# Local transformer: a new order of projections, scores, mixtures and gelus on the engines of one core

## The chip, the cores and the metric

The kernel runs on one core of a Trainium2 chip. The metric is the device time of one execution in microseconds (us), the median of several runs.

## The reference

Four layers, each x = x + s(LN(x)) * silu(g(LN(x))), with s an attention and g a feed-forward branch of many kinds. The change lies in the branch g of the first layer alone. That branch is itself a small transformer of 6 layers on 16 sequences of 256 tokens of 128 channels, with local attention:

```python
def attn_layer(x, Wqkv, qs, ksc, Wo):
    q, k, v = heads(x @ Wqkv)                 # 16 heads of 64
    q = l2norm(q) * qs; k = l2norm(k) * ksc
    q, k = rotary(q, scale), rotary(k, 1 / scale)
    out = local_attention(q, k, v)            # windows of 32 queries, 64 keys, softmax
    return out @ Wo

def ffn_layer(x, g, bln, W1, b1, W2, b2):
    hg = (layer_norm(x) * g + bln) @ W1 + b1
    a, gate = split(hg)                       # 341 + 341
    return a * gelu(gate) @ W2 + b2

for i in range(6):
    x = attn_layer(shift_tokens(x), ...) + x
    x = ffn_layer(shift_tokens(x), ...) + x
```

## The kernel before

The function local_transformer_stage works on tiles of 128 tokens: 32 tiles a layer, 192 in all, with all data in float32. It is one software pipeline. Each engine has its own instruction queue, written out as a loop over steps n; in step n, TensorE projects tile n, turns and scores tile n - 2, turns the probabilities of tile n - 3 and mixes it, and sends tile n - 4 through the output projection. Every fourth step carries a part of the feed-forward block for a group of 4 tiles: n mod 4 = 3 turn_rows and copy_rows, 0 the matmuls of gate and value with gelu (hidden, gelu, gate_hidden), 1 measure_rows, project_hidden and store_group. In odd steps turn_x and copy_x bring the input of the next two tiles.

The queues run in order and are joined by semaphores. What ties them around the change:

- A projection (project, L1127) goes in four units Q0, Q1, K0, K1 into a ring of two PSUM banks. ScalarE squares it (L1319), VectorE rotates it (L1522, L1526) and sums the squares (L1530); the bank is free when it is rotated. Gate and value matmuls (L1233) use the same ring.
- There is one PSUM bank for transposes (turn_bank). Each group of four transposes (L1135 for q and k, L1168 for probabilities, L1224 rows, L1117 x) waits until ScalarE has copied the group before it out (L1337, L1377, L1311).
- The scores (L1145 mask, L1158) of a tile fill two banks; VectorE takes the maxima (L1537) and subtracts them (L1542, shift_scores), ScalarE takes exp (L1348), VectorE sums (L1549), GpSimd multiplies by the reciprocals (L1482).
- The mixture (mix, L1183) is done in two pieces into the same two banks; ScalarE copies each piece to u (L1356), and project_out (L1195) multiplies u by the merged weights m, 16 heads of two passes each, into a bank of its own. A float32 matmul shows as two passes, each with a weight load.
- The norms' roots are taken by ScalarE (take_root: log L1342 and exp L1344) and refined by GpSimd (refine_root, L1464 to L1467); GpSimd also adds (L1450) and normalises (L1475).
- ScalarE changes its function table before the gelus (L1383) and back after them (L1390).

The projections and transposes use all 128 rows of TensorE's array; mask, scores and mixture work on halves of 64 rows.

## Time and profile before

| | us |
|---|---|
| median of 3 runs (lowest, highest) | 5391.65 (5387.35, 5395.55) |
| the profiled execution | 5392.81 |
| its span, first to last instruction | 5391.0 |
| TensorE matmuls busy, weight loads busy | 4720.6, 3338.6 |
| VectorE, ScalarE, GpSimd busy | 3708.4, 2807.9, 2810.1 |

Times of instructions are counted from the span's start. The mean clock that TensorE was granted over the span is 0.934 of full speed; in the stretch shown below it is 1.00. Matmuls are pipelined, so that the busy time of one instruction reaches into the next one; distances from start to start tell what a block costs.

### The profile page before, as it was taken

The page shows a single profiled execution, that of the slowest core. Times are in us where ns is not written, and L with a number is a line of the kernel's source. Part 1 is how long each engine was busy: PE and PEld are TensorE (multiplying, and loading weights), DVE is VectorE, ACT ScalarE, POOL GpSimd, SP SyncE. Part 2 cuts the span into 40 slices and gives each one's busy share as a digit, 9 for nine tenths or more (in the row PEclk, how much of TensorE's full clock was granted, in tenths as well). Part 3 has the DMA queues.
Part 4 walks back from the last instruction along what each step waited for, and adds up shares of the span by engine and source line. Part 5 has one row for each costly group of instructions (what it writes and reads, how often), then busy time and mean ns, then how long its engine had stood idle before and what let it go on. Part 6 is the DMA issues. An engine that isn't in the chain of part 4 may idle for free. (4 is left out here: it accounts for less than half of the span.)

```text
span 5391.0 us, 143191 instructions
## 1 busy us (share of the span) xinstructions
PE 4720.6 (88%) x57069; PEld 3338.6 (62%) x57103; DVE 3708.4 (69%) x8589; ACT 2807.9 (52%) x6208; POOL 2810.1 (52%) x3349
## 2 busy tenths in 40 slices
PE   7699999999999999999999999955375999845886
PEld 3367676666667767666676667744363667623665
DVE  7677777777777777777777777746725656577443
ACT  2266666666666666666666666621023666641342
POOL 4477776777677767776777777701122333311000
PEclk9799999999999999999999999977587999967898
DMA  0211111111111111111111110000211000010012
GB/s 21 66 35 25 25 35 37 25 25 33 32 29 25 35 31 29 25 35 33 29 25 34 22 28 21 18 24 2 77 52 24 2 2 2 1 25 13 26 29 58
DMA packets 312165, 150.62 MB, mean 28 GB/s; under 512 B 146143, under 2 KB 301004, under 8 KB 311244
## 3 DMA queue, kind: packets, MB, share of 16 engines
q1 hardware_dynamic: 309451, 137.20, 10.5%
q8 instruction: 461, 7.55, 0.6%
q0 software_dynamic: 2048, 4.20, 0.3%
q14 instruction: 205, 1.67, 0.1%
HBM read 101.10 MB, written 27.41 MB: 24 GB/s over the span
## 5 line engine op out<-in xcount | busy, mean ns | idle before, releaser
L1450 POOL TENSOR_TENSOR loc_a<-loc_a,loc_b 128x512 f32<-128x512 f32 x768 | 977.2, 1272 | 598.3 <-DVE loc_b L1526 598.3
L1127 PE MATMUL psum<-loc_wqk,loc_xt 128*128 128x512 f32 x1536 | 837.6, 628 | 12.3 <-DVE loc_b L1526 5.9
L1195 PE MATMUL psum<-loc_m,xn_rows 128*128 128x128 f32 x6144 | 843.7, 280 | 3.8 <-DVE y_rows L1558 2.6
L1475 POOL TENSOR_TENSOR loc_a<-loc_a,loc_rn 128x512 f32<-128x512 f32 x768 | 784.9, 1043 | 0.1
L1195 PEld LDWEIGHTS psum<-loc_m,xn_rows 128*128 128x128 f32 x6144 | 745.6, 192 | 55.9 <-issue 36.0
L1319 ACT ACTIVATE loc_sq<-psum 128x512 f32<-128x512 f32 x768 | 456.1, 594 | 449.6 <-PE psum L1127 443.2
L1522 DVE TENSOR_TENSOR loc_a<-psum,loc_rope 128x512 f32<-128x512 f32 x768 | 523.9, 682 | 174.9 <-ACT loc_sq L1319 161.7
L1356 ACT COPY xn_rows<-psum 128x512 f32<-128x512 f32 x768 | 412.3, 589 | 326.6 <-PE psum L1183 324.3
L1482 POOL TENSOR_TENSOR xn_cols<-xn_cols,loc_rec 128x512 f32<-128x512 f32 x384 | 392.3, 1042 | 307.5 <-DVE loc_rec L1553 307.5
L1135 PEld LDWEIGHTS psum<-ident,loc_a 128*128 128x128 f32 x3072 | 347.7, 142 | 317.9 <-issue 307.1
L1526 DVE TENSOR_TENSOR loc_b<-psum,loc_rope 128x512 f32<-128x512 f32 x768 | 520.8, 678 | 0.0
L1530 DVE TENSOR_REDUCE loc_n<-loc_sq 128x8 f32<-128x512 f32 x768 | 517.1, 673 | 0.0
L1135 PE MATMUL psum<-ident,loc_a 128*128 128x128 f32 x3072 | 477.0, 278 | 10.4 <-ACT loc_qt L1337 7.2
L769 POOL TENSOR_TENSOR l2a_p<-l2a_p,l2a_rec 128x256 f32<-128x256 f32 (+1 forms) x256 | 211.5, 826 | 441.5 <-DVE l2a_rec L756 441.5
L1183 PE MATMUL psum<-xn_cols,loc_x 64*128 64x256 f32 x3072 | 435.6, 402 | 1.1 <-ACT xn_rows L1356 0.9
L1537 DVE TENSOR_REDUCE loc_top<-psum 128x8 f32<-128x512 f32 x384 | 247.3, 686 | 236.7 <-PE psum L1158 236.7
L1337 ACT COPY loc_kt<-psum 128x512 f32<-128x512 f32 x384 | 224.7, 585 | 306.2 <-PE psum L1135 306.2
L1158 PE MATMUL psum<-loc_kt,loc_qt 64*32 64x64 f32 x24576 | 333.8, 223 | 3.2 <-issue 2.5
L1158 PEld LDWEIGHTS psum<-loc_kt,loc_qt 64*32 64x32 f32 x24576 | 295.0, 105 | 50.8 <-issue 39.6
L1168 PEld LDWEIGHTS psum<-ident,xn_cols 128*128 128x128 f32 x1536 | 181.2, 141 | 225.1 <-issue 225.1
L1127 PEld LDWEIGHTS psum<-loc_wqk,loc_xt 128*128 128x128 f32 x1536 | 232.7, 191 | 122.2 <-issue 59.7
L1183 PEld LDWEIGHTS psum<-xn_cols,loc_x 64*128 64x128 f32 x3072 | 264.4, 186 | 67.2 <-issue 10.4
(370 smaller groups left out, 8532.2 us busy)
## 6 DMA issues: line engine op xcount, KB each, us to landing
loc_x<-loc_shifted SPq DMA_DIRECT2D x192, 256.0 KB, 4.0
loc_shifted<-y_rows SPq DMA_DIRECT2D x144, 64.0 KB
loc_wqk<-in_L_ffn_Wqkv SPq DMA_DIRECT2D x24, 256.0 KB, 3.8
x_rows<-y_rows SPq DMA_DIRECT2D x96, 64.0 KB
x_rows<-y_rows SPq DMA_DIRECT2D x96, 63.5 KB
moe_w<-in_L_ffn_W SPq DMA_DIRECT2D x16, 256.0 KB, 5.0
l3a_qk<-l3a_rot SPq DMA_DIRECT2D x16, 256.0 KB, 2.1
grp_w<-in_L_ffn_W SPq DMA_DIRECT2D x16, 256.0 KB, 4.2
```

Source lines behind the costliest of these rows:

```text
L1127: nc.tensor.matmul(ring("p", i, unit), xt[:, b % 2, t * P:(t + 1) * P], wqk[:, unit * 512:(unit + 1) * 512], start=True, stop=True).then_i ...
L1135: last = nc.tensor.transpose(turn_bank[:, j * P:(j + 1) * P], a[:, (UNITS * i + unit) % (3 * UNITS), j * P:(j + 1) * P], core.ident[:, :])
L1158: last = nc.tensor.matmul(score_bank[h][32 * w:32 * w + 32, 64 * j:64 * j + 64], qt[rows_h, i % 2, j, 32 * w:32 * w + 32], kt[rows_h, b % ...
L1183: last = nc.tensor.matmul(u_bank[h][:, 256 * v:256 * v + 256], x2[rows_h, b % 3, WPT * t + w, :], pt[rows_h, i % 2, :, 32 * w:32 * w + 32] ...
L1195: last = nc.tensor.matmul(y_bank[:, 0:P], u[:, i % 2, h // 2, h % 2, :], m[:, h, :], start=(h == 0), stop=(h == HEADS - 1))
L1319: nc.scalar.activation(sq[:, g % 2, :], ring("p", i, unit), ACT.Square).then_inc(sem["squared"], 1)
L1356: nc.scalar.copy(to, u_bank[h].rearrange("p (w j q) -> p w j q", w=2, j=PAIRS)).then_inc(sem["u_copied"], 1)
L1450: nc.gpsimd.tensor_tensor(part, part, b_[:, g % 2, :], ALU.add).then_inc(sem["added"], 1)
L1475: nc.gpsimd.tensor_tensor(part, part, rn[:, i % 2, 8 * unit:8 * unit + 8].rearrange("p (h e) -> p h e", e=1).to_broadcast([P, 8, DH]), ALU ...
L1522: nc.vector.tensor_tensor(a[:, g % (3 * UNITS), :].rearrange("p (h d) -> p h d", d=DH), src.rearrange("p (h d) -> p h d", d=DH), cos, ALU. ...
L1526: nc.vector.tensor_tensor(b_[:, g % 2, :].rearrange("p (h s d) -> p h s d", s=2, d=32), halves, sin, ALU.mult).then_inc(sem["rotated"], 1)
L1530: nc.vector.tensor_reduce(n2[:, i % 2, 8 * unit:8 * unit + 8], sq[:, g % 2, :].rearrange("p (h d) -> p h d", d=DH), AX.X, ALU.add).then_in ...
```

## The change

The work is the same; its order on four queues changes, and one semaphore is split in two.

- TensorE: both projections of q stand first in a step. The output projection goes in four equal parts of 4 heads, three of them between the transposes of q and k, the last before the second mixture (before: 4, 4, 2 and 6 heads). The three gate and value pairs follow all transposes of q and k in one block. The second projection of k and the second transposes of the probabilities come ahead of the mask; the first mixture comes between the two halves of the scores. turn_rows, turn_values and turn_x now follow the scores.
- ScalarE: take_root comes ahead of the first copy of q, the gelu table is loaded ahead of the second copy of q, the three gelus follow all copies of q and k, and the first mixture is copied right after the second copy of the probabilities. The second mixture's copies are keep_mixed, with the semaphore u_kept.
- GpSimd: refine_root comes ahead of the probabilities' multiplies.
- VectorE: normalise_rows_of comes after the rotations of Q0 and Q1, shift_scores after that of K1.

```diff
+                    if piece == 1:
+                        pe.wait_ge(sem["u_copied"], 2 * (i + 1))
+                    elif i >= 1:
+                        pe.wait_ge(sem["u_kept"], 2 * i)
...
+                def project_out(i, part):
+                    if part == 0:
+                        pe.wait_ge(sem["u_copied"], 2 * (i + 1))
+                        pe.wait_ge(sem["u_kept"], 2 * (i + 1))
...
# TensorE, step n
                     if now(0):
                         project(n, Q0)
+                        project(n, Q1)
                     if now(2):
                         turn_qk(n - 2, "q", 0)
-                    if now(0):
-                        project(n, Q1)
+                    if now(4):
+                        project_out(n - 4, 0)
                     if now(2):
                         turn_qk(n - 2, "q", 1)
                     if now(4):
-                        project_out(n - 4, range(0, 4))
-                    if group_at(n, 12) is not None:
-                        hidden(group_at(n, 12), 0)
+                        project_out(n - 4, 1)
                     if now(2):
                         turn_qk(n - 2, "k", 0)
                     if now(4):
-                        project_out(n - 4, range(4, 8))
-                    if group_at(n, 12) is not None:
-                        hidden(group_at(n, 12), 1)
+                        project_out(n - 4, 2)
                     if now(2):
                         turn_qk(n - 2, "k", 1)
                     if group_at(n, 12) is not None:
-                        hidden(group_at(n, 12), 2)
+                        for c in range(CH):
+                            hidden(group_at(n, 12), c)
                     if now(0):
                         project(n, K0)
                     if now(3):
                         turn_probs(n - 3, 0)
-                    if now(2):
-                        mask_scores(n - 2)
-                        scores(n - 2, range(0, 4))
                     if now(0):
                         project(n, K1)
                     if now(3):
                         turn_probs(n - 3, 1)
                     if now(2):
+                        mask_scores(n - 2)
+                        scores(n - 2, range(0, 4))
+                    if now(3):
+                        mix(n - 3, 0)
+                    if now(2):
                         scores(n - 2, range(4, 8))
-                    if now(4):
-                        project_out(n - 4, range(8, 10))
                     if group_at(n, 11) is not None:
                         turn_rows(group_at(n, 11))
                     for half in range(2):
                         if starts(n, 1 + half) is not None:
                             turn_values(n // NT, half)
-                    if now(3):
-                        mix(n - 3, 0)
                     if n % 2 == 1 and n + 1 < TILES:
                         turn_x((n + 1) // 2)
                     if now(4):
-                        project_out(n - 4, range(10, 16))
+                        project_out(n - 4, 3)
                     if now(3):
                         mix(n - 3, 1)
...
# ScalarE, step n
                         square(n, Q0)
+                    if n - 1 in root_number:
+                        take_root(n - 1)
                     if now(2):
                         copy_turned("q", n - 2, 0)
-                    if n - 1 in root_number:
-                        take_root(n - 1)
                     if now(0):
                         square(n, Q1)
+                    if group_at(n, 12) is not None:
+                        nc.scalar.preload_act_table_set("gelu_and_others")
                     if now(2):
                         copy_turned("q", n - 2, 1)
...
                         copy_turned("p", n - 3, 1)
+                        copy_mixed(n - 3)
...
                         exps(n - 2, 0)
                         exps(n - 2, 1)
                     if now(3):
-                        copy_mixed(n - 3, 1)
+                        keep_mixed(n - 3)
...
# GpSimd, step n
                         clamp(n - 1)
+                        refine_root(n - 1)
                     if now(3):
                         normalise_probs(n - 3, 0)
                         normalise_probs(n - 3, 1)
-                    if n - 1 in root_number:
-                        refine_root(n - 1)
...
# VectorE, step n
-                    if group_at(n, 11) is not None:
-                        normalise_rows_of(group_at(n, 11))
                     if now(0):
                         rotate(n, Q0)
                         rotate(n, Q1)
+                    if group_at(n, 11) is not None:
+                        normalise_rows_of(group_at(n, 11))
...
                         rotate(n, K0)
+                        rotate(n, K1)
                     if now(2):
                         shift_scores(n - 2)
-                    if now(0):
-                        rotate(n, K1)
```

## Rows read from the trace of the kernel before

**Rows 1.** Stretches of four steps, their sum: busy us of each engine

```profile
sum 67.91, PE 67.72 PEld 47.61 DVE 52.66 ACT 42.59 POOL 49.07; mean PE 16.93 PEld 11.90 DVE 13.17 ACT 10.65 POOL 12.27
```

**Rows 2.** Timeline of TensorE's matmuls, end of step 1 and step 2: start, us, engine, line

```profile
2017.85 2.94 PE L1242 MATMUL psum<-loc_w,x_rows 128*128 128x128 f32 x24
2020.63 1.02 PE L1127 MATMUL psum<-loc_wqk,loc_xt 128*128 128x512 f32 x2
...
2024.32 0.61 PE L1135 MATMUL psum<-ident,loc_a 128*128 128x128 f32 x4
...
2025.70 0.63 PE L1135 MATMUL psum<-ident,loc_a 128*128 128x128 f32 x4
2026.16 1.02 PE L1127 MATMUL psum<-loc_wqk,loc_xt 128*128 128x512 f32 x2
2027.09 0.63 PE L1168 MATMUL psum<-ident,xn_cols 128*128 128x128 f32 x4
2027.65 0.41 PE L1145 MATMUL psum<-loc_window_mask,loc_pick 64*32 64x512 bf16 x8
2027.88 0.84 PE L1158 MATMUL psum<-loc_kt,loc_qt 64*32 64x64 f32 x64
...
2030.14 0.86 PE L1158 MATMUL psum<-loc_kt,loc_qt 64*32 64x64 f32 x64
2030.93 0.71 PE L1195 MATMUL psum<-loc_m,xn_rows 128*128 128x128 f32 x4
2031.57 1.14 PE L1183 MATMUL psum<-xn_cols,loc_x 64*128 64x256 f32 x8
2032.63 1.60 PE L1195 MATMUL psum<-loc_m,xn_rows 128*128 128x128 f32 x12
2034.17 1.14 PE L1183 MATMUL psum<-xn_cols,loc_x 64*128 64x256 f32 x8
```

**Rows 3.** Timeline of TensorE's weight loads, same step

```profile
2030.14 0.70 PEld L1158 LDWEIGHTS psum<-loc_kt,loc_qt 64*32 64x32 f32 x64 [0.17 <-issue]
...
2031.57 0.73 PEld L1183 LDWEIGHTS psum<-xn_cols,loc_x 64*128 64x128 f32 x8
```

**Rows 4.** Timeline of ScalarE, same step

```profile
2021.69 0.60 ACT L1319 ACTIVATE loc_sq<-psum 128x512 f32<-128x512 f32 x1 [2.50 <-PE psum L1127]
...
2023.07 0.58 ACT L1319 ACTIVATE loc_sq<-psum 128x512 f32<-128x512 f32 x1
2023.58 0.58 ACT L1337 COPY loc_qt<-psum 128x512 f32<-128x512 f32 x1
...
2032.75 1.07 ACT L1356 COPY xn_rows<-psum 128x512 f32<-128x512 f32 x2 [1.87 <-PE psum L1183]
2033.71 1.16 ACT L1348 ACTIVATE xn_cols<-xn_cols 128x512 f32<-128x512 f32 x2
```

**Rows 5.** Timeline of VectorE, step 2 and start of step 3

```profile
2027.85 0.69 DVE L1522 TENSOR_TENSOR loc_a<-psum,loc_rope 128x512 f32<-128x512 f32 x1 [1.07 <-ACT loc_sq L1319]
...
2031.04 1.29 DVE L1537 TENSOR_REDUCE loc_top<-psum 128x8 f32<-128x512 f32 x2 [1.30 <-PE psum L1158]
2032.24 1.28 DVE L1542 TENSOR_TENSOR xn_cols<-psum,loc_top 128x512 f32<-128x512 f32 x2
...
2036.91 2.69 DVE L1580 TENSOR_SCALAR loc_rows<-x_rows,loc_mv,loc_rn 128x128 f32<-128x128 f32 x4
```

**Rows 6.** Timeline of GpSimd and ScalarE, end of step 2 and step 3

```profile
2034.80 1.27 POOL L1450 TENSOR_TENSOR loc_a<-loc_a,loc_b 128x512 f32<-128x512 f32 x1 [0.72 <-DVE loc_b L1526]
...
2036.93 2.04 POOL L1482 TENSOR_TENSOR xn_cols<-xn_cols,loc_rec 128x512 f32<-128x512 f32 x2 [0.49 <-DVE loc_rec L1553]
...
2046.83 0.78 ACT L1377 ACTIVATE x_rows<-psum,loc_shift,loc_gain 128x512 f32<-128x512 f32 x1 [1.23 <-PE psum L1224]
```

**Rows 7.** Timeline of ScalarE, step 0: table load and the gelu behind it

```profile
2054.29 1.28 ACT L1383 ACT_TABLE_LOAD   x1
2055.58 0.69 ACT L1387 ACTIVATE x_rows<-psum,loc_b 128x512 f32<-128x512 f32 x1
```

More of the change, by code:

```diff
@@ L1185, in mix @@
                     last.then_inc(sem["u_done"], 1)
-                def project_out(i, heads):
-                    if heads.start == 0:
-                        pe.wait_ge(sem["u_copied"], 4 * (i + 1))
+                def project_out(i, part):
+                    if part == 0:
+                        pe.wait_ge(sem["u_copied"], 2 * (i + 1))
+                        pe.wait_ge(sem["u_kept"], 2 * (i + 1))
                         if i % NT == 0:
@@ L1193, in project_out @@
                             pe.wait_ge(sem["stored"], i)
-                    for h in heads:
+                    for h in range(4 * part, 4 * part + 4):
                         last = nc.tensor.matmul(y_bank[:, 0:P], u[:, i % 2, h // 2, h % 2, :], m[:, h, :], start=(h == 0),
                                                 stop=(h == HEADS - 1))
-                    if heads.stop == HEADS:
+                    if part == 3:
                         last.then_inc(sem["y_done"], 1)
@@ L1337, in copy_turned, with keep_mixed @@
                     nc.scalar.copy(to, turn_bank.rearrange("p (j q) -> p j q", j=4)).then_inc(sem["copied"], 1)
+                def keep_mixed(i):
+                    act.wait_ge(sem["u_done"], 2 * i + 2)
+                    for h in range(2):
+                        to = u[:, i % 2, :, h, 64:128].rearrange("p j (w q) -> p w j q", w=2)
+                        nc.scalar.copy(to, u_bank[h].rearrange("p (w j q) -> p w j q", w=2, j=PAIRS)).then_inc(sem["u_kept"], 1)
                 def take_root(i):
@@ L1348, in exps, with copy_mixed @@
                     nc.scalar.activation(probs[:, i % 2, :, h, :], probs[:, i % 2, :, h, :], ACT.Exp).then_inc(sem["exped"], 1)
-                def copy_mixed(i, piece):
-                    act.wait_ge(sem["u_done"], 2 * i + piece + 1)
-                    if i >= 2 and piece == 0:
+                def copy_mixed(i):
+                    act.wait_ge(sem["u_done"], 2 * i + 1)
+                    if i >= 2:
                         act.wait_ge(sem["y_done"], i - 1)
                     for h in range(2):
-                        to = u[:, i % 2, :, h, 64 * piece:64 * piece + 64].rearrange("p j (w q) -> p w j q", w=2)
+                        to = u[:, i % 2, :, h, 0:64].rearrange("p j (w q) -> p w j q", w=2)
                         nc.scalar.copy(to, u_bank[h].rearrange("p (w j q) -> p w j q", w=2, j=PAIRS)).then_inc(sem["u_copied"], 1)
@@ L1398, in _ @@
                         square(n, Q0)
+                    if n - 1 in root_number:
+                        take_root(n - 1)
                     if now(2):
                         copy_turned("q", n - 2, 0)
-                    if n - 1 in root_number:
-                        take_root(n - 1)
                     if now(0):
                         square(n, Q1)
+                    if group_at(n, 12) is not None:
+                        nc.scalar.preload_act_table_set("gelu_and_others")
                     if now(2):
                         copy_turned("q", n - 2, 1)
-                    if group_at(n, 12) is not None:
-                        gelu(group_at(n, 12), 0)
-                    if now(2):
                         copy_turned("k", n - 2, 0)
-                    if group_at(n, 12) is not None:
-                        gelu(group_at(n, 12), 1)
-                    if now(2):
                         copy_turned("k", n - 2, 1)
                     if group_at(n, 12) is not None:
-                        gelu(group_at(n, 12), 2)
+                        for c in range(CH):
+                            gelu(group_at(n, 12), c)
                     if now(0):
@@ L1429, in _ @@
                             copy_values(n // NT, half)
-                    if now(3):
-                        copy_mixed(n - 3, 0)
                     if n % 2 == 1 and n + 1 < TILES:
```

6 lines of the change are left out of this document (1 added, 5 removed).

## The prediction

> **What bounds the kernel now.** The diff touches the local transformer alone. I read the page first, then stretches of that stage: in four steps that repeat (steps with n mod 4 = 1, 2, 3, 0 in turn) TensorE is busy 67.72 of 67.91 us, VectorE 52.66, GpSimd 49.07, ScalarE 42.59 [rows 1]. Then the timeline of each engine in these steps. The reader is to see there that TensorE's blocks start without a hole, each when the one before it has streamed [rows 2], so that what counts on TensorE is the distance from one start to the next, and that it is the other engines that wait. All starts below are such differences.
>
> Prices on TensorE [rows 2]: a projection takes 0.93 (K0, 2026.16, to the next block, 2027.09); four transposes 0.46 (2025.70 to 2026.16); from one group of transposes to the next, with one output block of 8 passes and the copy out of the one turn bank between them, 1.38 (2024.32 to 2025.70). Changing between blocks that use all 128 rows and blocks on halves of 64 rows costs extra: transposes into the mask matmuls 0.56 instead of 0.46; 4 passes of the output projection into a mixture 0.64, 12 passes 1.54, so 0.11 a pass and 0.19 for the change; a mixture and the way out of it 1.06; half of the scores and the way out 0.79.
>
> **The change, part by part.** No instruction is added or removed. The semaphore's split, the parts' numbering and the extra TensorE wait on the second mixture's copies cost nothing by themselves. What changes is order, on four engines.
>
> *TensorE's gain.* Before, the half-row blocks stand in three places: mask and first scores (then K1), second scores (then output), each mixture alone. After, mask, scores, first mixture, scores are one run. Of the four ways in and four ways out, two of each are left. How dear the changes inside that run are, no row shows. Floor: the weight loads alone, 0.70 for 64 score loads and 0.73 for the mixture's eight, 1.43 together [rows 3]. Ceiling: both with a full way out, 0.79 + 1.06 = 1.85 [rows 2]. I take 1.6, near the middle, since the two blocks use the same two halves but differ in columns. The Trainium skill (TensorE: Matmul & The Clock Gate, Part 3, The mechanism) says that weight loads overlap running matmuls only when their row groups differ; by that, alternating halves hide the loads and the floor holds, which would take 33 us off my time; no run here shows it.
>
> *One step after, without extras.* Time 0 is the start of VectorE's rotation of K0 (2027.85), 1.69 after K0's matmul (2026.16) [rows 2, 5]. K0 -1.69, first probabilities' transposes -0.76, K1 -0.30, second transposes 0.63, mask 1.19, scores 1.42 (mask block 0.23), second scores 1.42 + 1.6 = 3.02. From there TensorE goes on: last output part 3.81, second mixture 4.90 (0.64 + 4 passes), next step's Q0 5.96, Q1 6.89, first transposes of q 7.82, and it would like the second ones at 7.82 + 1.38 = 9.20.
>
> But these second transposes wait for ScalarE's copy of the first, and that copy now stands at the end of a line. The scores are done 0.90 after their start (2030.14 to 2031.04) [rows 2, 5], at 3.92; that VectorE now rotates K1 (three instructions, 0.60 apart as the two maxima are: 2031.04 to 2032.24) ahead of them costs nothing, since two rotations end at 3.58. The first shifted half is ready 1.20 + 0.68 later, 5.80, the second at 6.40 [rows 5]. On ScalarE the two exps follow, the second from 6.43 to 7.06 (0.63: two overlap to 1.16); then, in its order, both copies of the second mixture, 0.96 to the next start (2032.75 to 2033.71), so the square of Q0 starts at 8.04 [rows 4]. Square, copy, log and exp take 1.38 from start to the next square (2021.69 to 2023.07); with the root taken first the copy is last, and as an instruction that reads PSUM ends 0.11 after the next could start (2032.75 + 1.07 against 2033.71), 9.53 [rows 4]. TensorE gets the bank 0.15 later (2023.58 + 0.58 to the transposes at 2024.32) [rows 2, 4], 9.68 instead of 9.20. Before, the scores were done much earlier in the step and this line was over when Q0 ended. From 9.68: two turns of 1.38, 0.46, 1.69: the next rotation of K0 at 14.59. TensorE alone would have given 14.11.
>
> *The step with project_hidden (1 to 2).* TensorE: transposes of x at 3.81 (two, 0.23), output 4.04, mixture 5.13, project_hidden 6.19, 2.78 long (2017.85 to 2020.63) [rows 2], Q0 8.97, q's transposes 10.83, three turns of 1.38, 0.46, 1.69: 17.1. ScalarE's line is hidden under the 2.78; without them it would cost the 0.48 here too.
>
> *The steps with rows and hidden (2 to 3 to 0).* Four things. First, turn_rows is now followed by turn_x at once, and that waits for copy_rows: transposes at 3.81, done 0.63 later, copy 0.78 [rows 6], bank free at 5.39 instead of 4.27: 1.12 of TensorE, which the first mixture covered before. Second, normalise_rows goes behind both rotations of Q. Its four tensor_scalars take 2.69 and the first two of them end with GpSimd's two multiplies of 2.04 together that run beside them [rows 5, 6]; behind the rotations GpSimd runs adds of 1.27 and multiplies of about 1.02 without a break, so I expect one tensor_scalar for each of these: 3.5 to 4.6, I take 4.0. From 8.67 (square of Q0 done) two rotations of 1.79 and 4.0 give 16.25 against 14.59, but step 0 takes it up: the shift starts at 1.66 + 3.58 = 5.24 in place of 3.92, and so q's first copy ends at 10.85, where TensorE, 1.12 late itself, would take the bank at 11.01 (Q0 7.77, q 9.63). At 4.6 it would cost 0.5. Third, the load of the gelu table, 1.28 [rows 7], stands ahead of the copy that frees the bank: square 0.51 (2023.07 to 2023.58) [rows 4], load 1.28, copy 0.58, 2.37 in place of 1.39 (hand-over 0.15, transposes 0.63 and 0.03, copy 0.58): 0.98 of TensorE that was spent beside projections before. Fourth, the six gate and value matmuls come in one block after all of k's transposes; at 0.93 each, 5.58, which holds some waits for gelu and for the product. So from step 3: 10.85 + 2.37 + 0.15 + 1.38 + 0.46 + 5.58 + 1.69, 22.5 with rounding. Two steps: 14.6 + 22.5 = 37.1.
>
> The load: after its 1.28 the gelu starts 0.01 later (2054.29, 2055.58) [rows 7]. The Trainium skill (ScalarE: Activation LUTs, What ACT_TABLE_LOAD costs) gives 2.66 us a switch, a drain of 1.38 included; by that the moved load would add another 65 us. The row decides; no drain shows.
>
> *GpSimd* now waits for the root (square, log and exp, which is the 1.38 without the copy: about 8.95) before its probabilities; they are wanted at 13.83, and four small operations and 2.04 fit between. Without that room turn_probs would be late. No DMA moves: the queue's order is as before, and windows and shifted rows wait on counts that come no later in a step.
>
> *Sum.* 14.6 + 17.1 + 37.1 = 68.8 us for four steps, against 67.91 [rows 1]: +0.9. There are 48 such groups, 47 after the start: +42. Once in each of 6 layers turn_values stands ahead of turn_x as turn_rows does, about 0.9: +5. On the profiled execution's 5392.8 (span 5391.0 and 1.8 around it; 1.2 over the median) that gives 5440 us.
>
> **Rivals.** *TensorE alone sets the pace (faster).* Every wait above is hidden as all are now. Then two steps of 14.11, 17.12, and 20.4 for step 0 (22.5 less 1.12 and 0.98): 65.7, -2.2 for four steps, -103: 5290 us. For it: slack of 15 us and more in 68 on the other engines [rows 1]. Against it: the lines are made of latencies, not of load. It decides where the copy of q's first half is back within 5.28 us after the last score; I count 5.76 with the hand-over.
> *The gains and the waits cancel (same).* The run of scores and mixture at its floor (-0.17 a step, -33 us), and besides ScalarE's line 0.1 shorter than I add it up (-19 over 192 steps): 5388. For it: the loads overlap within the scores already [rows 3]. Against it: both are needed.
> *Dearer still.* That run at its ceiling (+0.25 a step, +48) and normalise_rows at 4.6 (+0.5 in four steps, +24): 5512. The two ends of the unknown costs are thus 5407 and 5512.
>
> **Numbers.** Forecast, slower between 5407 and 5512: 0.68. Faster rival and what lies between it and the kernel before: 0.15. Same: 0.13. Beyond 5512: 0.04. About 0.2%, 11 us, is what a measurement can tell from no change. The range leaves out the faster rival and the dearest end: 5382 to 5512; the forecast's own is 5407 to 5512. Faster 0.15, same 0.13, slower 0.72.
>
> **What would show it.** In the profile after: in a plain step ScalarE goes from the exps through the copies of the mixture to the square without a hole, and TensorE waits some 0.5 us before the second transposes of q; before turn_x in step 3, 1.1 us; after the table load, 1 us at k's first transposes; the tensor_scalars near 1 us each. Four steps of 68.8 us. If TensorE shows no such holes and four steps take under 67, the line from the last score to the copy was counted too long, and the prediction is wrong there; if plain steps take 15, the run of scores and mixture is dearer.

## The result and the profile after

The changed kernel takes 5551.39 us (median of 4 runs, 5543.07 to 5556.7) against 5393.47 before on the same chip: a ratio of 1.0292, 95% interval 1.0276 to 1.0308. It is slower by 2.9%, some 158 us, where 0.9%, 47 us, was forecast, and it lies above the range. Ratios below are all to the kernel before, each with its runs on one chip; differences between two experiments are differences of these ratios times 5392. A ratio is known to some 0.16%, 9 us, and so the difference of two experiments to some 13 us.

The page of the kernel after, its head and two groups of its part 5:

```profile
span 5541.3 us, 143200 instructions
...
PE 4740.0 (86%) x57069; PEld 3332.4 (60%) x57103; DVE 3786.4 (68%) x8589; ACT 2858.3 (52%) x6208; POOL 2800.9 (51%) x3349
...
L1520 DVE TENSOR_TENSOR loc_a<-psum,loc_rope 128x512 f32<-128x512 f32 x768 | 525.1, 684 | 303.6 <-ACT loc_sq L1318 298.4
...
L1158 PEld LDWEIGHTS psum<-loc_kt,loc_qt 64*32 64x32 f32 x24576 | 296.6, 105 | 107.3 <-issue 96.8
```

The same work is done and all engines have room; the loads of the scores stand idle 96.8 us for "issue", that is for nothing that the profile shows as a wait. In the page of the kernel before it is 39.6:

```profile
L1158 PEld LDWEIGHTS psum<-loc_kt,loc_qt 64*32 64x32 f32 x24576 | 295.0, 105 | 50.8 <-issue 39.6
```

Most of both is regular: 0.17 ahead of the second half of a tile's scores before [rows 3], 33 us in 192 steps, and 0.33 at the same place after (shown below), 63 us. The rest, 7 and 33 us, stands in single steps; such a stretch in which TensorE stands still without a wait is called a hole below. Starts measure holes best: where a half of the scores takes longer to the next block than it does at its shortest, the excess over all 384 halves sums to 11 us before and 38 us after. This sum is called the late halves from here on.

The granted clock in the steps below is 1.00, the upper of the two levels, as before.

Stretches of four steps (n mod 4 = 1, 2, 3, 0), the counterpart of [rows 1]:

```profile
2361.31:2379.30 17.99, 17.84 (x244) 13.50 (x243) 13.27 (x30) 12.09 (x24) 12.20 (x15) 1.00 0.13 31
2379.30:2394.39 15.09, 14.85 (x219) 10.52 (x217) 11.74 (x21) 7.41 (x15) 12.19 (x15) 1.00 0.12 28
2394.39:2410.57 16.18, 15.22 (x224) 11.12 (x222) 15.71 (x25) 10.44 (x22) 12.19 (x15) 1.00 0.15 35
2410.57:2432.00 21.43, 20.40 (x230) 12.37 (x228) 13.62 (x24) 13.70 (x24) 12.29 (x15) 1.00 0.03 8
sum 70.69, PE 68.31 PEld 47.52 DVE 54.34 ACT 43.64 POOL 48.87; mean PE 17.08 PEld 11.88 DVE 13.58 ACT 10.91 POOL 12.22
```

70.69 where 68.8 was forecast. TensorE now stands idle for long in two of the four steps, 0.96 in the third and 1.03 in the fourth. Averaged over the middle steps of the layers (starts of Q0 in the trace) four steps went from 68.10 to 71.04: 17.71, 14.65, 15.41, 20.32 became 17.90, 15.04, 16.69, 21.40. The first five steps of a layer went from 94.25 to 99.45 (mean of the last five layers).

Timeline of TensorE in steps 2 and 3, the counterpart of [rows 2]:

```profile
2381.31 0.60 PE L1135 MATMUL psum<-ident,loc_a 128*128 128x128 f32 x4
2382.13 1.13 PE L1198 MATMUL psum<-loc_m,xn_rows 128*128 128x128 f32 x8 [0.22 <-DVE y_rows L1556]
2383.10 0.60 PE L1135 MATMUL psum<-ident,loc_a 128*128 128x128 f32 x4
...
2389.43 0.84 PE L1158 MATMUL psum<-loc_kt,loc_qt 64*32 64x64 f32 x64
2390.20 1.13 PE L1185 MATMUL psum<-xn_cols,loc_x 64*128 64x256 f32 x8
2391.26 0.86 PE L1158 MATMUL psum<-loc_kt,loc_qt 64*32 64x64 f32 x64
2392.05 1.45 PE L1198 MATMUL psum<-loc_m,xn_rows 128*128 128x128 f32 x8
...
2406.76 0.66 PE L1227 MATMUL psum<-ident,loc_rows 128*128 128x128 f32 x4
2408.38 0.41 PE L1117 MATMUL psum<-ident,y_rows 128*128 128x128 f32 x2 [0.96 <-ACT x_rows L1382]
```

First scores to mixture 0.77 (2389.43 to 2390.20), mixture to second scores 1.06: 1.83 for what was taken as 1.6. From turn_rows to turn_x 1.62 (2406.76 to 2408.38); 1.58 was forecast. And a wait that the prediction does not have: the output's first part, now between q's two transposes, starts 0.82 behind the first of them instead of 0.46, because VectorE has not yet added the output of the tile before (y_rows).

Timeline of the weight loads in another step 3, the counterpart of [rows 3]:

```profile
2262.76 0.73 PEld L1185 LDWEIGHTS psum<-xn_cols,loc_x 64*128 64x128 f32 x8
2263.82 0.55 PEld L1158 LDWEIGHTS psum<-loc_kt,loc_qt 64*32 64x32 f32 x46 [0.33 <-issue]
2264.94 0.25 PEld L1158 LDWEIGHTS psum<-loc_kt,loc_qt 64*32 64x32 f32 x18 [0.57 <-issue]
```

0.33 of nothing between the mixture's loads and the scores', and then, after 46 of 64 score loads, a hole of 0.57 inside the block, ended by no semaphore. From the second scores to the next block the mean is 0.95 to 1.05 by the block that follows, the median 0.79 (from starts, 181 blocks); over all 192 tiles the mean is 0.985, and 0.84 in the kernel before.

ScalarE and VectorE around steps 2, 3 and 0, the counterparts of [rows 4, 5 and 7]:

```profile
2394.08 1.23 ACT L1353 ACTIVATE xn_cols<-xn_cols 128x512 f32<-128x512 f32 x2 [1.62 <-DVE xn_cols L1540]
2395.21 1.05 ACT L1342 COPY xn_rows<-psum 128x512 f32<-128x512 f32 x2
2396.15 0.61 ACT L1318 ACTIVATE loc_sq<-psum 128x512 f32<-128x512 f32 x1
2396.64 0.24 ACT L1347 ACTIVATE loc_log<-loc_n 128x36 f32<-128x36 f32 x1
2396.92 0.23 ACT L1349 ACTIVATE loc_root<-loc_log 128x36 f32<-128x36 f32 x1
2397.06 0.57 ACT L1336 COPY loc_qt<-psum 128x512 f32<-128x512 f32 x1
...
2414.61 1.28 ACT L1409 ACT_TABLE_LOAD   x1
2415.91 0.58 ACT L1336 COPY loc_qt<-psum 128x512 f32<-128x512 f32 x1
```

```profile
2379.61 0.69 DVE L1596 TENSOR_TENSOR y_rows<-psum,y_rows 128x512 f32<-128x512 f32 x1 [2.72 <-PE psum L1245]
2380.22 1.27 DVE L1547 TENSOR_REDUCE loc_total<-xn_cols 128x8 f32<-128x512 f32 x2
...
2381.76 0.23 DVE L1556 TENSOR_TENSOR y_rows<-psum,y_rows 128x128 f32<-128x128 f32 x1
...
2400.38 4.62 DVE L1578 TENSOR_SCALAR loc_rows<-x_rows,loc_mv,loc_rn 128x128 f32<-128x128 f32 x4
...
2408.51 1.27 DVE L1535 TENSOR_REDUCE loc_top<-psum 128x8 f32<-128x512 f32 x2
```

```profile
2400.43 1.26 POOL L1449 TENSOR_TENSOR loc_a<-loc_a,loc_b 128x512 f32<-128x512 f32 x1
2401.65 1.04 POOL L1474 TENSOR_TENSOR loc_a<-loc_a,loc_rn 128x512 f32<-128x512 f32 x1
2402.65 1.27 POOL L1449 TENSOR_TENSOR loc_a<-loc_a,loc_b 128x512 f32<-128x512 f32 x1
2403.89 3.04 POOL L1474 TENSOR_TENSOR loc_a<-loc_a,loc_rn 128x512 f32<-128x512 f32 x3
```

In step 2 VectorE stands 2.72 us until project_hidden is done (L1245), then sums the probabilities (L1547), and only then adds the output of the tile before (2381.76 to 2381.99). TensorE's first output part, which waits for that add, starts at 2382.13. In the step 3 shown the add (which ends at 2396.53) holds nothing up; on the mean of steps 1 and 3 the output's first part starts 0.66 behind q's first transposes, 0.20 late. ScalarE's line from the exps through the kept copies to q's first copy runs without a hole, as foretold. The table load stands ahead of q's second copy, and the copy starts 0.02 after it. The four tensor_scalars take 4.62, the far end of the 3.5 to 4.6 that were considered: they end (2405.00) with the fourth of the GpSimd instructions that run beside them without a break, add, multiply, add and multiply. The maxima of that step's scores start at 2408.51, 1.75 after the block behind the scores began (2406.76).

### The profile page after: what moved, and what is told of

It is laid out like the page before. It is cut to its first block and busy times, and to the rows that moved or that the text cites. A ratio compares the mean times of both kernels' runs of the same rounds, so it can differ in the third digit from the quotient of the medians.

```text
span 5541.3 us, 143200 instructions
## 1 busy us (share of the span) xinstructions
PE 4740.0 (86%) x57069; PEld 3332.4 (60%) x57103; DVE 3786.4 (68%) x8589; ACT 2858.3 (52%) x6208; POOL 2800.9 (51%) x3349
## 3 DMA queue, kind: packets, MB, share of 16 engines
q8 instruction: 461, 7.55, 0.6%
## 5 line engine op out<-in xcount | busy, mean ns | idle before, releaser
L1127 PE MATMUL psum<-loc_wqk,loc_xt 128*128 128x512 f32 x1536 | 788.7, 613 | 10.8 <-ACT loc_m L1373 4.6
L1463 POOL TENSOR_TENSOR loc_tmp<-loc_root 128x36 f32<-128x36 f32 x194 | 47.7, 246 | 814.9 <-ACT loc_root L1349 814.9
L1127 PEld LDWEIGHTS psum<-loc_wqk,loc_xt 128*128 128x128 f32 x1536 | 245.7, 192 | 197.9 <-issue 129.9
L1158 PEld LDWEIGHTS psum<-loc_kt,loc_qt 64*32 64x32 f32 x24576 | 296.6, 105 | 107.3 <-issue 96.8
L1158 PE MATMUL psum<-loc_kt,loc_qt 64*32 64x64 f32 x24576 | 340.8, 223 | 23.5 <-issue 22.2
L1353 ACT ACTIVATE xn_cols<-xn_cols 128x512 f32<-128x512 f32 x384 | 235.1, 630 | 234.4 <-DVE xn_cols L1540 233.9
L1361 ACT COPY xn_rows<-psum 128x512 f32<-128x512 f32 x384 | 206.2, 589 | 285.9 <-PE psum L1185 285.9
L1168 PEld LDWEIGHTS psum<-ident,xn_cols 128*128 128x128 f32 x1536 | 164.7, 140 | 270.0 <-issue 270.0
```

The costliest lines, as they stand in the source:

```text
L1127: nc.tensor.matmul(ring("p", i, unit), xt[:, b % 2, t * P:(t + 1) * P], wqk[:, unit * 512:(unit + 1) * 512], start=True, stop=True).then_i ...
L1158: last = nc.tensor.matmul(score_bank[h][32 * w:32 * w + 32, 64 * j:64 * j + 64], qt[rows_h, i % 2, j, 32 * w:32 * w + 32], kt[rows_h, b % ...
```

## The experiments

**Four parts undone singly.** All on the changed kernel.

ScalarE's order of root and first copy:

```diff
-                    if n - 1 in root_number:
-                        take_root(n - 1)
                     if now(2):
                         copy_turned("q", n - 2, 0)
+                    if n - 1 in root_number:
+                        take_root(n - 1)
```

> ScalarE copies the first half of q's transposes out of PSUM ahead of the root's log and exp, as the kernel before does; all else as in the changed kernel. Theory A, that ScalarE's line from the last score to this copy sets a plain step: the copy comes back about 0.8 us earlier, the wait ahead of q's second transposes (now 0.36 us over the unblocked turn) goes, and 0.3 to 0.4 us of some 100 to 140 steps are saved: about 5505 us, 35 to 55 less than the changed kernel. Theory B, that the time is lost inside TensorE's run of scores, mixture and scores: the hole moves elsewhere and the time stays within 10 us of the changed kernel's. GpSimd's root comes 0.6 later, which neither theory prices.

Measured: 5530.48 us, 1.0266 (1.0249 to 1.0283), 14 us less than the changed kernel; the two intervals overlap, so that the times alone hardly show a gain, and neither theory's size came. Steps 1 and 3 are 0.16 and 0.17 shorter (17.66 to 17.50, 16.47 to 16.30 at their commonest), steps 2 not at all (14.80). So the line is real but short: the wait ahead of q's second transposes in step 3 (1.09 from the output's first part, 0.93 where nothing is waited for) goes, and the one ahead of the output's first part itself stays (0.66 behind q's first transposes instead of 0.46, before and after this edit). At the table load the turn grows from 1.93 to 2.32, so that part of what is won is waited for again there.

The place of the table load:

```diff
-                    if group_at(n, 12) is not None:
-                        nc.scalar.preload_act_table_set("gelu_and_others")
                     if now(2):
                         copy_turned("q", n - 2, 1)
+                    if group_at(n, 12) is not None:
+                        nc.scalar.preload_act_table_set("gelu_and_others")
+                    if now(2):
                         copy_turned("k", n - 2, 0)
```

> The gelu table is loaded behind the second copy of q instead of ahead of it. Theory A, that the load's place costs the 1.0 us by which k's first transposes are late in every fourth step (2.40 us from q's second transposes, 1.39 elsewhere): the load now stands in the turn after, ahead of k's first copy, beside the same four passes, and so the same 1.0 us should show at k's second transposes, less what ScalarE was ahead by, 0.1 to 0.5: between 0 and 25 us less than the changed kernel. Theory B, that the step is set by VectorE, which rotates Q0 and Q1 behind normalise_rows: no change beyond 5 us.

Measured: 5525.89, 1.0258 (1.0241 to 1.0275), 18 us less. From starts, the 1.93 ahead of k's first transposes went back to 0.93 and the next turn grew to 1.43: a stall of 1.0 became one of 0.5 one turn later, as expected; 0.5 in 47 steps is 23 us.

The first mixture behind scores and rows:

```diff
-                    if now(3):
-                        mix(n - 3, 0)
                     if now(2):
                         scores(n - 2, range(4, 8))
                     if group_at(n, 11) is not None:
                         turn_rows(group_at(n, 11))
...
+                    if now(3):
+                        mix(n - 3, 0)
# ScalarE: copy_mixed(n - 3) likewise behind copy_rows and copy_values
```

> The scores are undivided again and the first mixture stands behind turn_rows and turn_values, ahead of turn_x, as in the kernel before; its copy likewise. All other edits of the change stay. Theory A, waits: the wait between turn_rows and turn_x goes (1.1 us in 47 steps, 52 us), and the scores end 1.06 us earlier, which shortens ScalarE's line in plain steps (0.3 to 0.4 us in some 140 steps, 40 to 55 us): about 5450 us. Theory B, the way in and out of the blocks: the run of scores, mixture and scores costs 1.84 us where undivided scores and a mixture by itself would cost 1.8 to 1.9; by that alone nothing is won but the 52 us: about 5500. If TensorE's long second halves of the scores (mean about 1.0 us instead of 0.84) come from the dense run of short instructions, they stay or become longer, since the run gets no shorter.

Measured: 5554.93, 1.0312 (1.0295 to 1.0329): nothing won, and neither theory holds. The wait at turn_x did go (turn_rows to the next block 0.64 instead of 1.62), and with it 1.0 of step 3. It came back in two places: step 0 went from 21.4 to 22.1, waiting for VectorE and ScalarE behind the late tensor_scalars, and the undivided scores have large holes (late halves 98 us). The timeline of the weight loads in one step, and the DMA strip of the microseconds 938 to 942 in 40 slices:

```profile
938.31 1.48 PEld L1158 LDWEIGHTS psum<-loc_kt,loc_qt 64*32 64x32 f32 x126
941.54 0.13 PEld L1158 LDWEIGHTS psum<-loc_kt,loc_qt 64*32 64x32 f32 x2 [1.76 <-issue]
...
DMA  0000000080000000000000000000000000000000
...
q8 instruction: 1, 0.02, 2.1%
```

With two of 128 score loads to go TensorE stands still for 1.76 us. The only transfer near is one of the queue that brings instructions; it begins at 938.8 (the ninth slice), and the hole ends 2.7 later. Of the 55 holes of over 0.5 us between score instructions in this trace every one ends 2.2 to 3.0 us behind the start of such a transfer (start of the instruction behind the hole, less that of the last transfer begun before it). So do all 48 and all 60 such holes in two other kernels with undivided scores (the one edit on the kernel before, and the four things undone, both below), 2.2 to 2.9 us behind a start, although these transfers start 10 us apart on the median.

VectorE's normalisation of the rows:

```diff
+                    if group_at(n, 11) is not None:
+                        normalise_rows_of(group_at(n, 11))
                     if now(0):
                         rotate(n, Q0)
                         rotate(n, Q1)
-                    if group_at(n, 11) is not None:
-                        normalise_rows_of(group_at(n, 11))
```

> VectorE normalises the rows ahead of the rotations of Q0 and Q1 again. My prediction says that its later place is taken up by step 0, whose TensorE is late itself by the wait at turn_x: within 10 us of the changed kernel. The rival, that the four tensor_scalars beside GpSimd's adds and multiplies hold up the next shift of the scores: 0.3 to 0.5 us in 47 groups of four steps, 15 to 25 us less.

Measured: 5524.1, 1.0246 (1.0229 to 1.0263), 25 us less. My claim that step 0 takes it up falls; the rival holds. The group of the tensor_scalars in the kernel after, and in this one, total and mean ns of one:

```profile
L1578 DVE TENSOR_SCALAR loc_rows<-x_rows,loc_mv,loc_rn 128x128 f32<-128x128 f32 x192 | 215.0, 1178 | 0.0
```

```profile
L1578 DVE TENSOR_SCALAR loc_rows<-x_rows,loc_mv,loc_rn 128x128 f32<-128x128 f32 x192 | 53.7, 343 | 0.1
```

The same 192 instructions take 3.4 times as long beside GpSimd's tensor operations.

**The scores' neighbours.** The holes of the last but one experiment made a theory: TensorE runs out of instructions where many short ones follow each other. Four kernels tested it and what is left without the change's waits. Mask and first scores ahead of K1 again:

```diff
+                    if now(2):
+                        mask_scores(n - 2)
+                        scores(n - 2, range(0, 4))
                     if now(0):
                         project(n, K1)
                     if now(3):
                         turn_probs(n - 3, 1)
-                    if now(2):
-                        mask_scores(n - 2)
-                        scores(n - 2, range(0, 4))
                     if now(3):
                         mix(n - 3, 0)
```

> The mask and the first half of the scores stand ahead of K1 and of the second transposes of the probabilities again, as before the change; the first mixture stays between the halves of the scores. Theory S, that TensorE runs out of instructions where mask, scores, mixture and scores follow each other (holes with no wait ahead of score instructions, 119 us in the changed kernel): with a projection and four transposes in the middle the holes shrink to those of the kernel before, 40 to 50 us less, while the second way into half rows (0.56 instead of 0.46) costs 0.10 in 192 steps, 19 us: about 5525 us. Theory W, that only the ways in and out of half rows and waits for other engines count: 19 us more than the changed kernel, about 5570.

Measured: 5651.98, 1.0478 (1.046 to 1.0495), 100 us more: neither theory. The edit was ill chosen, as TensorE's timeline shows:

```profile
2096.35 0.60 PE L1168 MATMUL psum<-ident,xn_cols 128*128 128x128 f32 x4
2097.68 1.14 PE L1185 MATMUL psum<-xn_cols,loc_x 64*128 64x256 f32 x8 [0.72 <-ACT xn_cols L1336]
```

The mixture needs ScalarE's copy of the second transposes of the probabilities, and the mask and first scores had covered that copy: 1.33 instead of some 0.55, 0.78 in 192 steps, 150 us. For the holes it is clear all the same: second scores to the next block is 0.79 in every kind of step, the late halves sum to 1 us, and the four steps became regular (18.55, 15.69, 17.36, 21.80 again and again). 150 of wait less some 40 of holes is about the 100 measured, if the second way into half rows is left aside.

The same edit on the kernel with the mixture behind the scores:

> The mixture behind the undivided order of scores, as in the experiment that moved it, and besides the mask and first scores ahead of K1 and of the second transposes. Theory S: in the experiment with the mixture behind the scores, holes with no wait took 167.5 us ahead of score instructions; here K1 and the transposes break the run, the holes fall to some 50 to 70 us, and one more pair of ways in and out costs 0.24 in 192 steps, 46 us: about 5495 us, 60 less than that experiment's 5555. Theory W: no holes to win, 46 us more, 5600.

Measured: 5533.84, 1.0261 (1.0243 to 1.0278), 27 us less than with the scores undivided, between the two theories. The holes went as theory S has it: the late halves fell from 98 to 10 us. The idle time for "issue" that the expectations of this section go by (here 167.5 us, and 42.0 measured) is the sum of the view of line L1158; it adds the weight loads' idle time to the matmuls', so that one hole counts nearly twice, and it holds the regular 0.17. By the late halves 88 us of holes are gone for 46 of ways, which would leave 42. Step 0 went on waiting (22.4).

Four things undone together: the edits of the first, third and fourth experiment, and the gate and value pairs back between k's transposes, with the table load among them.

> Of the changed kernel four things are undone together: q's first copy ahead of the root, the first mixture behind scores and rows, gate and value pairs with their gelus and the table load spread between k's transposes, and normalise_rows ahead of the rotations. Q0 and Q1 first, the output projection in four parts, K1 and both transposes of the probabilities ahead of mask and undivided scores stay. Theory S: the undivided scores keep their holes, 90 us and more, so that it does not fall below the kernel before: 5420 to 5480 us. Theory W: each undone wait gives back what it cost (52, 18, 45 and 24 us of 5551): about 5410, and below 5391 if the shorter ways in and out count as well.

Measured: 5464.89, 1.013 (1.0113 to 1.0147), 87 us less than the changed kernel and inside theory S's range. The late halves are 112 us (192.0 in the view).

And with mask and first scores ahead of K1 besides:

> The four things undone, and besides mask and first scores ahead of K1 and of the second transposes again. What stays of the change: both projections of q first, the output projection in four equal parts, refine_root first on GpSimd, VectorE's shift behind K1's rotation. Theory S: 40 to 60 us less than with the four things alone, since the holes go; 5380 to 5430 us. Theory W: 46 us more than with the four things alone, 5440 to 5500.

Measured: 5405.48, 1.0025 (1.0016 to 1.0035). One edit, 57 us less, as theory S has it, and the late halves fall from 112 to 9 us (192.0 to 41.4 in the view). Theory W had this edit cost 46. What remains of the change costs 0.25%: in plain steps (15.17) the second mixture starts 1.33 behind the last output part instead of 1.09, since eight passes do not cover the copy of the first mixture, and the output's first part still waits for y_rows in step 2 (0.82 instead of 0.46).

**One part of the change alone, on the kernel before.**

```diff
+                    if now(0):
+                        project(n, K1)
+                    if now(3):
+                        turn_probs(n - 3, 1)
                     if now(2):
                         mask_scores(n - 2)
                         scores(n - 2, range(0, 4))
-                    if now(0):
-                        project(n, K1)
-                    if now(3):
-                        turn_probs(n - 3, 1)
-                    if now(2):
                         scores(n - 2, range(4, 8))
```

> The kernel before with one edit of the change alone: K1 and the second transposes of the probabilities stand ahead of the mask, so that mask and all scores are one run. Theory W (ways in and out alone): one pair less, 0.53 + 0.77 against 0.46 + 0.60, 0.24 us in 192 steps, 46 us less than before, 5345. Theory S (TensorE runs out of instructions in a long run of score matmuls): holes with no wait ahead of score instructions grow from the 42 us of the kernel before to 165 to 190 us, as in the two kernels with undivided scores; with the 46 us gained this ends 75 to 100 us slower than before, 5465 to 5490.

Measured: 5455.97, 1.0127 (1.0106 to 1.0148), 68 us more, where theory S had 75 to 100 more. The view of the score matmuls' line in this kernel, with the idle time ahead of them (us, times):

```profile
L1158 PE MATMUL psum<-loc_kt,loc_qt x24576: 212/216/241, 250.6 to 3582.3; 64*32 64x64 f32 x200
...
  issue: 142.1, 101
```

and in the kernel before:

```profile
  issue: 42.0, 223
```

142.1 is 73.8 of the loads, as the list of groups has it,

```profile
L1158 PEld LDWEIGHTS psum<-loc_kt,loc_qt 64*32 64x32 f32 x24576 | 281.0, 105 | 84.3 <-issue 73.8
```

and 68.3 of the matmuls in the same holes, some 50 of them; the 42.0 before are nearly all the regular 0.17. From starts the late halves grow from 11 to 82 us. Both terms are to be seen: a plain step without a hole is 14.33, 0.27 less than the 14.60 of the kernel before, as the shorter ways have it, and single steps of 15.7 to 16.0 stand between. The way gained is real in steps 1 and 2, and the holes take it and more. In step 3 K1 starts 0.32 later than elsewhere.

The kernels of this section side by side: the late halves, and the four kinds of step from K0 to K0 (last five layers, without the first five steps of each), their medians and their means added up. The median is a step without a hole, so that mean less median is what the holes cost.

| kernel | late halves, us | four steps, medians | means |
|---|---|---|---|
| before | 11 | 67.90 | 68.09 |
| before, one run of scores | 82 | 67.60 | 69.56 |
| changed | 38 | 70.46 | 71.06 |
| changed, mixture behind the scores | 98 | 69.90 | 71.07 |
| the same, mask and first scores early | 10 | 70.86 | 70.94 |
| four things undone | 112 | 67.69 | 69.53 |
| the same, mask and first scores early | 9 | 68.00 | 68.12 |

In the kernel before the one edit wins 0.30 of ways in four steps, where 0.96 was hoped for, and loses 1.77 to holes: 1.47 in 47 groups, 69 us, is the 68 measured.

**The block of gates.** On the changed kernel:

```diff
# TensorE: hidden(..., 0), (..., 1) ahead of k's first and second transposes, (..., 2) behind them
-                        for c in range(CH):
-                            hidden(group_at(n, 12), c)
# ScalarE
+                    if now(2):
+                        copy_turned("q", n - 2, 1)
                     if group_at(n, 12) is not None:
                         nc.scalar.preload_act_table_set("gelu_and_others")
+                        gelu(group_at(n, 12), 0)
                     if now(2):
-                        copy_turned("q", n - 2, 1)
                         copy_turned("k", n - 2, 0)
# and gelu(..., 1), gelu(..., 2) each behind a copy of k
```

> Of the changed kernel only the block of gate and value pairs is undone: the pairs and their gelus stand between k's transposes again, the table load behind q's second copy. By my prediction's terms the load's place costs 0.98 us in 47 steps, 46 us, and the block nothing by itself; the experiment that moved the load alone gave 22 us less. So 5505 to 5530 if that is all of it. Rival: the block also costs because gelus and products wait for each other without transposes between them (5.68 us where the pairs between transposes take 1.72, 1.72 and 1.80, 0.43 more): about 45 us less, 5505.

Measured: 5485.55, 1.0178 (1.016 to 1.0197), 61 us less, more than either reckoning. Each had one term only: the load's 0.98 and the block's 5.58 against 1.72 + 1.72 + 1.80 are together 1.32 in 47 steps, 62 us.

**What the run of half-row blocks is worth without its price.** On the kernel before, the output's part of two heads goes behind the first mixture, so that scores and mixture touch:

```diff
-                    if now(4):
-                        project_out(n - 4, range(8, 10))
...
-                        project_out(n - 4, range(10, 16))
+                        project_out(n - 4, range(8, 16))
```

> The kernel before with the two heads of the output projection that stand between the scores and the first mixture moved behind that mixture (8 heads there in place of 6), so that scores and mixture follow each other without a change to full rows: the idea of the change without a longer run of scores. Theory W: 0.79 + 0.64 + 1.06 + 1.53 becomes 0.79 + 1.06 + 1.97, 0.2 us less in some 140 steps, 0.1 or less in the 46 with turn_rows between: 25 to 35 us less than before, about 5363. Theory S: the run of half-row instructions grows by the mixture's 16 only, with a projection and four transposes ahead of it, so the holes stay near 42 us and the gain is the same; were the holes to grow by 30 us, the time would be that of before.

Measured: 5369.49, 0.9963 (0.9951 to 0.9974), 20 us less than before, where 25 to 35 were expected; the late halves stay at 11 us (43.3 in the view, 42.0 before). And in the steps with gates the change's order of Q1 and output besides (where `gates` is group_at(n, 12) is not None):

```diff
+                    if now(0) and gates:
+                        project(n, Q1)
                     if now(2):
                         turn_qk(n - 2, "q", 0)
-                    if now(0):
+                    if now(4) and gates:
+                        project_out(n - 4, range(0, 4))
+                    if now(0) and not gates:
                         project(n, Q1)
                     if now(2):
                         turn_qk(n - 2, "q", 1)
                     if now(4):
-                        project_out(n - 4, range(0, 4))
+                        project_out(n - 4, range(4, 8) if gates else range(0, 4))
```

> The same, and in the steps with the gates both projections of q first and the output's first 8 heads ahead of the first gate matmul, as the changed kernel has them. In the kernel before, the first pair waits for the gelu (2.14 us to the next transposes against 1.72); with all of the change's waits undone and this order, the step took 19.87 instead of 20.32. Expected: 0.45 us in 46 steps, 20 us less than the kernel with the joined mixture alone, about 5343; rival: the gain is given back in the step after by VectorE, and the time stays at that kernel's.

Measured: 5348.22, 0.9923 (0.9907 to 0.9939): 42 us less than before and 22 less than with the joined mixture alone, as expected; the fastest here. TensorE's timeline of a plain step's end and of a step with gates:

```profile
1937.91 0.86 PE L1158 MATMUL psum<-loc_kt,loc_qt 64*32 64x64 f32 x64
1938.71 1.13 PE L1183 MATMUL psum<-xn_cols,loc_x 64*128 64x256 f32 x8
1939.77 2.05 PE L1195 MATMUL psum<-loc_m,xn_rows 128*128 128x128 f32 x16
1941.75 1.13 PE L1183 MATMUL psum<-xn_cols,loc_x 64*128 64x256 f32 x8
...
1961.99 1.06 PE L1195 MATMUL psum<-loc_m,xn_rows 128*128 128x128 f32 x8
1962.88 1.88 PE L1233 MATMUL psum<-x_rows,loc_w 128*128 128x512 f32 x4
1964.60 0.60 PE L1135 MATMUL psum<-ident,loc_a 128*128 128x128 f32 x4
```

Scores, mixture, eight heads, mixture: 0.80 + 1.06 + 1.98, where it was 0.79 + 0.64 + 1.06 + 1.54. The first gate pair takes 1.72 (1962.88 to 1964.60); its gelu is no longer waited for.

## Why the prediction was too small

The direction and most mechanisms were right; the step that failed is the first, "Floor ... Ceiling ... I take 1.6", the run of scores, mixture and scores. It was mis-sized in two ways, and a third term, normalise_rows, went to its far end.

1. **The ways inside the run.** 0.77 + 1.06 = 1.83 in place of 1.6, so the ceiling of 1.85: going from the mixture to the scores (a way is the extra time for such a change of shape) costs the same 1.06 as going to full rows. 0.23 or 0.24 in 192 steps are 45 us. The rule that I set beside the floor (the Trainium skill, TensorE: Matmul & The Clock Gate, Part 3, The mechanism: loads overlap only matmuls of other row groups) does not give the floor here: 0.33 stands empty between the mixture's loads and the scores' although both alternate between two halves; their columns differ (64*128 and 64*32). The measurement decides; why the stretch is empty no run shows.
2. **Holes in the instruction stream.** Not in the prediction at all, which bounded the run by its ways only, though the trace before has them small (35 of 384 halves late, 11 us in all). The second scores took 0.985 to the next block on the mean, 0.79 without a hole; the late halves are 38 us, 27 more than before. The clean tests are the two pairs with one edit: on the kernel before, late halves from 11 to 82 us and 68 us slower; with the four things undone, from 112 to 9 us and 57 us faster. That a long run of scores makes the holes is shown. That they are waits for an instruction transfer is read from where they end (163 of 163 at 2.2 to 3.0 us behind the start of one); no run took the transfers away.
3. **normalise_rows.** 4.62 in place of 4.0, and not taken up by step 0: 25 us by the experiment. The prediction's own rule, one tensor_scalar for each of GpSimd's adds (1.27) and multiplies (1.02), gives 4.58; it took 4.0 without a reason.

With the 47 that were forecast these make 45 + 27 + 25 + 47 = 144 of the 158 us. A wait that was put at nothing stands beside them: in the step with project_hidden the first turn takes 1.79 in place of 1.38, for y_rows, which is 0.41 in 47 steps, 19 us. Smaller misses go either way, and the terms are not quite independent, so that the sum shows only that no large term is missing.

The other steps, counted from K0 to K0 as the prediction counts them. *Plain steps, 14.59:* 14.88 and 14.96 on the mean, where the run alone should have given 14.8 and its holes 15.0, but the wait is of another kind in part. The wait of 0.48 that I put ahead of q's second transposes is 0.16 there, in step 3; another 0.20 in that step and 0.36 in step 2, which I had thought free, stand ahead of the output's first part, which waits for VectorE's y_rows. The change moves that part ahead of the second transposes, and I costed the move without listing what it waits for. *The step with project_hidden, 17.1:* 18.01, by the run, its holes and the y_rows above. *Steps 3 to 0, 22.5:* 23.21. *turn_rows to turn_x:* 1.58 foretold, 1.62. *Table load:* 2.37 to k's first transposes foretold, 2.40 (2414.24 to 2416.64 in the trace); no drain shows behind the load (1.28, then 0.02), against the 2.66 of the Trainium skill (ScalarE: Activation LUTs, What ACT_TABLE_LOAD costs). *Gate block:* 5.58 foretold, 5.68. *GpSimd's root first at no cost:* no run speaks against it, but none moved it alone. The sign named for a dearer run, plain steps of 15, is what came.

The rival "dearer still" (5512) had the first and the third of these and gave them 0.04; what lies beyond it is the holes. I gave it so little because I took a bound on TensorE's cost from blocks that stood apart; the run that the change makes is longer than any in the trace before.

## What to carry to other kernels

Putting like blocks together saves their changeover, but look at how many instructions the joined run issues in how short a time: here 128 score matmuls with their loads in 1.4 us were too many, and a projection and four transposes in their middle, which seemed to cost 0.24 us a step, paid for themselves. When a block is moved ahead, list every semaphore it waits for, not only that of the block it was meant to cover; twice here (the output's first part, and my own experiment with the early scores) the forgotten one decided. A wait removed in one step is worth nothing until the next engine in line is known: of the 1.0 us at turn_x two thirds went straight to step 0.

## What the runs showed of the hardware

- One queue brings instructions in 461 transfers of 16 KB, 7.55 MB. If all of them are TensorE's, which no row names but the holes suggest, its 114172 matmuls and loads come some 248 to a transfer (an estimate). 128 score matmuls and their loads take 1.39 us from start to the next block, while a hole of over 0.5 us between score instructions ends 2.2 to 3.0 us after the start of a transfer (163 holes in three kernels). The longest was 2.0 us in the kernel with the mixture behind the scores.
- VectorE's tensor_scalar of 128x128 takes 343 ns with no GpSimd tensor operation beside it; the mean of a group of four is 712 where two stand beside GpSimd's multiplies (kernel before), and 1178 where all four stand beside its adds and multiplies (changed kernel).
